# Delta heads: three runs of projections per slot, keys projected after the gate, a last merge level of 64 columns, weight turns moved

## The chip, the core and the metric

The kernel runs on one core of one Trainium2 chip. The metric is the device time of the whole kernel in microseconds (us), as the median of several runs. Times inside an execution are read from one profiled execution.

## What is computed

The program is one decoder layer of three blocks: a gated delta-rule attention, a cross attention and a feed-forward block with experts. The change touches the first block alone, and in it the part that runs over the heads. Cut to what matters here, the reference of it is

```
q = silu(conv4(x @ Wq.T)); k = silu(conv4(x @ Wk.T)); v = silu(conv4(x @ Wv.T))
g = exp(-exp(A_log) * softplus(x @ Wa.T + dt_bias)); beta = sigmoid(x @ Wb.T)
q = q / norm(q); k = k / norm(k)          # per head, 16 heads of 128
for t in time:                            # S is 128 x 128 per head and sequence
    e = v[t] - g[t] * (k[t] @ S)
    S = g[t] * S + outer(k[t], beta[t] * e)
    o[t] = q[t] @ S
o = rmsnorm(o) * norm_w * silu(x @ Wg.T)
return o @ Wo.T
```

There are 4 sequences of 512 tokens and 16 heads. The kernel does not step through time. It cuts time into 4 chunks of 128 tokens, and in each chunk solves a triangular system: with L the 128 x 128 lower triangle of scaled key products, it needs the inverse of (1 + L), once per head, chunk and sequence.

## The kernel before

**Slots.** `delta_heads` is a software pipeline of slots. Slot (i, c) finishes chunk c of head i for all 4 sequences at once, and beside it prepares later chunks. There are 3 slots that only fill the pipeline, a loop over the heads 0 to 14 with 4 slots each, and 4 slots of the last head. Each engine has its own in-order program of the slot, in the function `slot` of its block, and the engines meet in counting semaphores. So the order in which calls stand in each `slot` is the order of the work; no planner changes it. n = 4i + c numbers the slots.

**Projections.** x @ W for one chunk and one of the four weights (K, V, Q, G) is `project` (L526): 128 x 512 outputs (128 channels, 4 sequences of 128 tokens), 4 blocks of the input width, and 3 matmuls per block, because x and W are split into a leading and a remaining part; 12 matmuls in all. K and V share one bank of `gd_PJ`, Q and G share the other (`W_BANK`). Slot n projects K for chunk n + 2, and Q, V and G for chunk n + 1. ACT copies a result out and starts the convolution (`copy_pre`, two instructions), DVE adds the three other taps (`tap`), ACT applies silu (`silu`). For K, DVE then takes the squared norms (`gd_diag`, `gd_kss`), ACT the root (`gd_klen`), DVE the scales, and DVE makes the triangle `gd_Lo`. In the kernel before, K and Q are each projected in two runs of 6 matmuls, V in runs of 3 and 9, G in one run of 12, with other work between.

**The inverse.** Blocks of 16 x 16 on the diagonal are inverted on POOL (`solve`). They go there and back by DMAs on SP's queue: store the triangle, fetch its blocks (`fetch_blocks`, L458), solve, write T and W (the inverse and its transpose), and load them (`spread`). Then three merge levels with block sizes 16, 32 and 64 complete the inverse. A level l is a chain over PE and DVE:

`spread_rows(l)` on PE (W by Lo into bank 2), `masked(l)` on DVE (gives Y), `merge(l)` on PE (Y by T into bank 3), `merged(l)` on DVE (adds into W), and for l < 2 `turn_inverse(l)` on PE (transposes W) and `inverse_rows(l)` on DVE (updates T).

All three levels use the full 128 x 128 Lo and T as the stationary operand, and 64 moving columns.

**The rest of a slot** on PE: `ks` (S by k), `oi` (S by q), `u` (W by R, the corrected values; R is made on DVE from ks and the scaled values Vb), the transposes of v, q and k, `kk` and `qk` (key and query products), `o_sum` and `s_sum` (output and new state), the transpose of o. In slots c = 0 there is no old state, so ks, oi and R are missing.

**Weights.** SP loads the raw weights of the next head. PE transposes them (`turn_weights`, 4 transposes into the bank of that weight), ACT takes the leading part (`lead_weights`), DVE the rest (`rest_weights`), and only then is the bank free and the weight usable. Before, K is turned near the end of slot c = 1, V near the end of c = 2, Q early in c = 3 and G near the end of c = 3, just before the G projection that uses it.

**Two lines that a reader of the trace needs.** An f32 matmul of two f32 operands is recorded as two instructions, so that a group over the 4 sequences reads x8 (a transpose reads x4). Helpers hold the lines: L533 is every projection matmul, L543 every product of `each`, L548 every transpose of `turned`, L524 the turning of weights.

Of the kernel before, what the change touches and what calls it, by code (L numbers as in the profile page):

```python
# [5 lines left out]
ALU = mybir.AluOpType  # L6
# [6 lines left out]
P = 128  # L13
# [307 lines left out]
NM = len(MERGE)  # L321
MERGE_AT = NLV - NM


def delta_heads(nc, xn_parts, A, const_dram, ptab, osq, og_dram, lo_dram, images_dram, rows_dram):
# [10 lines left out]
    with ExitStack() as ctx:  # L336
# [182 lines left out]
        def _(pe):  # L519
# [7 lines left out]
            def project(j, cm, ks, done):  # L527

                bank = PJ[:, W_BANK[j], :].rearrange("p (b t) -> p b t", b=B)
                for k in ks:  # L530
# [4 lines left out]
                    if k == KT - 1:  # L535
                        mm.then_inc(done, 1)
# [14 lines left out]
            def slot(i, c, back, has1, has2, has3, more):  # L551
                n = i * CH + c
                par, parm = c % 2, (c + 1) % 2
                h2, c2 = (i if c < 2 else i + 1), (c + 2) % CH
                h1, c1 = (i if c < 3 else i + 1), (c + 1) % CH
                k_c, q_c, k_m, q_m = of(kT, par), of(qT, par), of(kT, parm), of(qT, parm)
# [3 lines left out]
                def spread_rows(l):  # L560
# [6 lines left out]
                    each(half[2], tiles(Lo_c), [second(W_c, MERGE[l])[:, b] for b in range(B)], y_sum)  # L567

                def merge(l):
# [5 lines left out]
                    each(half[3], tiles(T_c), [Y[:, l % 2, b, :] for b in range(B)], wup)  # L575
# [7 lines left out]
                if back:  # L583
                    spread_rows(0)
                if has2:
                    pe.wait_ge(v_pre, n + 3)
                    pe.wait_ge(w_copied, h2 * 4 + JK + 1)
                    if c == CH - 1:
                        pe.wait_ge(w_copied, h1 * 4 + JV + 1)
                    project(JK, c2, (0, 1), k_proj)  # L590
                if back and c > 0:
                    pe.wait_ge(s_ready, n + 1)
                    each(Bk[1], k_c, tiles(S), ks_done)
                if back:
                    merge(0)
                if has2:
                    project(JK, c2, (2, 3), k_proj)
# [3 lines left out]
                if back:  # L601
                    pe.wait_ge(v_silu, n + 1)
                    pe.wait_ge(kd_ready, n + 1)
                    turned(Bk[5], [vT[:, b * P:(b + 1) * P] for b in range(B)], v_turned)
                    turn_inverse(0)
                    spread_rows(1)
                if has1:
                    pe.wait_ge(g_silu, n + 2)
                    pe.wait_ge(w_copied, h1 * 4 + JQ + 1)
                    project(JQ, c1, (0, 1), q_proj)  # L610
                if back:
                    merge(1)
                if has1:
                    project(JQ, c1, (2, 3), q_proj)
                if back:
                    turn_inverse(1)
# [5 lines left out]
                if back:  # L622
                    spread_rows(2)
# [2209 lines left out]
```

## Time and profile before

| | us |
|---|---|
| median of 3 runs | 3859.66 (3859.34 to 3862.22) |
| the profiled execution, its own time | 3863.27 |
| span of the profiled execution | 3861.5 |
| stage of the delta heads in it (157 to 1840 of the span) | 1683 |
| PE busy over the span | 3359.5 (87%) |
| DVE, ACT, POOL busy | 2143.7 (56%), 1850.7 (48%), 1540.3 (40%) |

The profile is one execution. Its own time is 3.6 us over the median of the runs shown. Busy shares are averages over stages with different limits, and matmuls overlap in the record, so a busy PE is not yet a PE at its peak. PE is the matmul, PEld the loading of its stationary operand; the time from the start of one matmul group to the start of the next says what the group costs.

### The profile page before, as it was taken

The numbers are of one execution on the slowest core, as the hardware profiler recorded it, in microseconds if no ns is written. First come the engines' busy times: TensorE is split into PE (matmuls) and PEld (weight loads), VectorE is DVE, ScalarE is ACT, GpSimd is POOL, SyncE is SP. The second block draws the span as 40 slices with busy tenths as digits, with TensorE's granted clock in tenths as the row PEclk, the third lists the DMA queues.
The fourth block names the chain that finished last, engine by engine and source line by source line (L and its number), as shares of the span: only waits on it lengthen the run. The fifth ranks groups of instructions, "written<-read, shape, count | busy, mean of one in ns | idle before, by whom it ended". The sixth has DMA issues, their size and how long they took to land. (4 is left out here: it accounts for less than half of the span.)

```text
span 3861.5 us, 61617 instructions
## 1 busy us (share of the span) xinstructions
PE 3359.5 (87%) x19269; PEld 2648.6 (69%) x19300; DVE 2143.7 (56%) x4562; ACT 1850.7 (48%) x4568; POOL 1540.3 (40%) x3055
## 2 busy tenths in 40 slices
PE   3699999999999999999894788699969999964993
PEld 2588888888888888888672444388846667653441
DVE  3476676676676676665325677555454644621223
ACT  2466666666666666665210455434433534531110
POOL 2567677667667667674001000155540000003103
PEclk9799999999999999999897899899989999985996
DMA  2222222222222222221443100133362021034325
GB/s 53 77 65 61 69 54 60 70 64 61 70 64 61 70 63 61 66 57 40 153 131 139 61 14 14 39 96 112 100 234 94 27 76 54 33 130 164 123 89 159
DMA packets 432119, 311.55 MB, mean 81 GB/s; under 512 B 131392, under 2 KB 348608, under 8 KB 430816
## 3 DMA queue, kind: packets, MB, share of 16 engines
q1 hardware_dynamic: 424544, 288.99, 25.0%
q0 software_dynamic: 5120, 16.78, 1.3%
q10 hardware_dynamic: 2304, 4.20, 0.3%
q14 instruction: 108, 0.88, 0.1%
q8 instruction: 43, 0.70, 0.1%
HBM read 195.99 MB, written 113.90 MB: 80 GB/s over the span
## 5 line engine op out<-in xcount | busy, mean ns | idle before, releaser
L533 PE MATMUL gd_PJ<-xn_lead,gd_w_rest 128*128 128x512 f32 x1024 | 443.8, 433 | 20.5 <-DVE gd_w_rest L687 20.5
L533 PE MATMUL gd_PJ<-xn_lead,gd_w_lead 128*128 128x512 f32 x1024 | 405.6, 396 | 0.0
L533 PE MATMUL gd_PJ<-xn_rest,gd_w_lead 128*128 128x512 f32 x1024 | 401.8, 392 | 0.0
L694 DVE SCALAR_TENSOR_TENSOR gd_conv<-gd_pre,gd_cur_a,gd_conv 128x512 f32<-128x512 f32 x384 | 298.0, 776 | 90.3 <-ACT gd_conv L842 83.5
L959 POOL TENSOR_TENSOR gd_T<-gd_T,gd_prod 32x14 f32<-32x14 f32 (+6 forms) x896 | 305.8, 341 | 70.2
L956 POOL TENSOR_TENSOR gd_prod<-gd_L,gd_T 32x14 f32<-32x14 f32 (+6 forms) x896 | 299.7, 334 | 70.2
L533 PEld LDWEIGHTS gd_PJ<-xn_lead,gd_w_rest 128*128 128x128 f32 x1024 | 195.4, 191 | 51.0 <-DVE gd_w_rest L687 26.1
L533 PEld LDWEIGHTS gd_PJ<-xn_lead,gd_w_lead 128*128 128x128 f32 x1024 | 193.4, 189 | 45.6
L2505 POOL MEMSET ms_rank<- 128x1 f32 x8 | 0.3, 98 | 554.7 <-POOLq L55 554.7
L533 PEld LDWEIGHTS gd_PJ<-xn_rest,gd_w_lead 128*128 128x128 f32 x1024 | 195.6, 191 | 26.3
L543 PEld LDWEIGHTS gd_B<-gd_Y,gd_T 128*128 128x128 f32 x1536 | 196.2, 191 | 15.4 <-issue 4.1
L2215 PE MATMUL sa_B<-sa_kT,sa_qT 128*128 128x512 f32 (+3 forms) x512 | 179.2, 473 | 30.9 <-DMA sa_qT<-turned_queries_keys 18.0
L2279 ACT ACTIVATE sa_E<-sa_B,sa_nmax 128x512 f32<-128x512 f32 (+3 forms) x256 | 132.4, 525 | 151.8 <-DVE sa_nmax L2329 151.8
L543 PE MATMUL gd_B<-gd_W,gd_Lo 128*128 128x64 f32 x1536 | 195.0, 270 | 7.5 <-DMA gd_T<-inverse_image 7.3
L543 PEld LDWEIGHTS gd_B<-gd_W,gd_Lo 128*128 128x128 f32 x1536 | 187.5, 192 | 10.4 <-issue 7.5
L543 PE MATMUL gd_B<-gd_Y,gd_T 128*128 128x64 f32 x1536 | 193.8, 269 | 0.5 <-DVE gd_Y L707 0.5
L841 ACT COPY gd_pre<-gd_PJ 128x512 f32<-128x512 f32 x192 | 111.9, 583 | 163.6 <-PE gd_PJ L533 156.6
L713 DVE TENSOR_TENSOR gd_W<-gd_W,gd_B 128x256 f32<-128x256 f32 x192 | 80.5, 419 | 190.5 <-PE gd_B L543 190.1
L1452 POOL TENSOR_TENSOR xt_xt<-x_xres,x_bpb 128x512 f32<-128x512 f32 x16 | 20.4, 1281 | 367.7 <-DVE xt_y L1668 306.9
L1860 PE MATMUL sp_B<-sp_w_lead,sp_h_rest 128*128 128x512 f32 x384 | 157.2, 409 | 11.3 <-POOL sp_h_rest L1991 11.3
L2265 PE MATMUL sa_B<-sa_wo_lead,sa_o_parts 128*128 128x512 f32 x512 | 158.7, 390 | 8.9 <-issue 8.9
L694 DVE SCALAR_TENSOR_TENSOR gd_conv<-gd_pre,gd_cur_k,gd_conv 128x512 f32<-128x512 f32 x192 | 146.8, 765 | 16.2 <-ACT gd_conv L842 13.8
(401 smaller groups left out, 8839.2 us busy)
## 6 DMA issues: line engine op xcount, KB each, us to landing
turned_queries_keys<-f_wq SPq DMA_DIRECT2D x16, 1280.0 KB, 6.0
gd_row_sums<-decay_sums SPq DMA_DIRECT2D x64, 256.0 KB, 3.6
triangles<-gd_Lo SPq DMA_DIRECT2D x64, 256.0 KB, 3.4
gd_W<-turned_image SPq DMA_DIRECT2D x64, 256.0 KB, 2.8
gd_T<-inverse_image SPq DMA_DIRECT2D x64, 256.0 KB, 3.3
gated_outputs<-gd_og SPq DMA_DIRECT2D x64, 256.0 KB, 2.7
go_ogt<-gated_outputs SPq DMA_DIRECT2D x16, 1024.0 KB, 6.8
sa_qT<-turned_queries_keys SPq DMA_DIRECT2D x16, 1024.0 KB, 5.6
```

The lines of the kernel that those rows point to most:

```text
L533: mm = pe.matmul(bank, w_parts[wp][:, j, k, :], rhs, start=(k == 0 and wp == 1), stop=(k == KT - 1 and wp + xp == 0))
L543: mm = pe.matmul(bank[:, b, :], lhs[b], rhs[b], start=True, stop=True)
L694: nc.vector.scalar_tensor_tensor(out=conv[:, j], in0=pre[:, parm, j, :, d:d + P], scalar=cur[:, 4 * j + d:4 * j + d + 1], in1=conv[:, j], ...
L713: nc.vector.tensor_tensor(second(W_c, s), second(W_c, s), half[3].rearrange("p b (g m) -> p b g m", m=s), ALU.add).then_inc(w_ready, 1)
L841: nc.scalar.copy(pre[:, parm, j, :, 3:3 + P], bank)
L956: nc.gpsimd.tensor_tensor(prod[:, rows, 0:j], L16[:, rows, j:j + 1].to_broadcast(shape), T16[:, j:j + 1, 0:j].to_broadcast(shape), ALU.mul ...
L959: nc.gpsimd.tensor_tensor(T16[:, rows, 0:j], T16[:, rows, 0:j], prod[:, rows, 0:j], ALU.subtract).then_inc(solving, 1)
L1452: nc.gpsimd.tensor_tensor(xt[:, par, :], xres[:, bass.ds(t, 1), :].rearrange("p o d -> p (o d)"), bpb[:, :], ALU.add).then_inc(bias_ready, 1)
L1860: mm = pe.matmul(bank[:, :], h_parts[hp][:, s, k, :], w_parts[wp][:, k, j, :], start=(k == 0 and hp == 1), stop=(k == KT - 1 and hp + wp = ...
L2215: pe.matmul(Bk[bank][:, col:col + w], qT[:, h, i * P:(i + 1) * P], kT[:, h // REP, 0:w], start=True, stop=False)
L2265: mm = pe.matmul(Bk[i][:, :], part(o_parts, h, op)[:, i * P:(i + 1) * P], wo_parts[wp][:, h, :], start=(h == 0 and op == 1), stop=(h == HE ...
L2279: ex = nc.scalar.activation(E[:, par, E_AT[i]:E_AT[i] + w], Bk[bank][:, col:col + w], ACT.Exp, bias=nmax[:, par, i:i + 1], accum_out=sums[ ...
```

## The change

Nothing is computed otherwise. The parts are:

1. **Three runs of projections per slot.** Q and V are each projected in one run of 12. K moves to right behind G, so that G and K make one run of 24. In slot n it is then for chunk n + 3; ACT's copy of it stays where it was, at the start of a slot, so it is now done in slot n + 1.
2. **The last merge level has 64 columns.** For l = 2 only the lower left 64 x 64 block is new. So the stationary operands are cut to 64 columns (`Lo_c[:, b, 0:TOP]`, `T_c[:, b, 0:TOP]`), PE writes 64 partitions, DVE's `masked(2)` is a multiplication by -1 and `merged(2)` a copy, both of 64 partitions and still 256 elements each.
3. **Weight turns moved.** Q to the very start of slot c = 3, K from the end to the middle of c = 1 (behind the Q projection), G from the end to the middle of c = 3 (before the V projection). V stays at the end of c = 2. ACT's and DVE's parts move with them.
4. **Order of the rest.** On PE the transpose of q now stands before `u`. On DVE the first two taps of K stand between `masked(0)` and `merged(0)`, the first tap of Q comes before `gd_diag`, and `merged(2)` comes after the scales. On ACT the root of the key norms comes before `oi`, and the V copy before the copy of U.

The diff, cut to its core:

```diff
+TOP = MERGE[-1]
...
-            def project(j, cm, ks, done):
+            def project(j, cm, done):
...
+                h3, c3 = (i if c < 1 else i + 1), (c + 3) % CH
...
-                    each(half[2], tiles(Lo_c), [second(W_c, MERGE[l])[:, b] for b in range(B)], y_sum)
+                    if l < NM - 1:
+                        each(half[2], tiles(Lo_c), [second(W_c, MERGE[l])[:, b] for b in range(B)], y_sum)
+                    else:
+                        each(half[2][0:TOP], [Lo_c[:, b, 0:TOP] for b in range(B)], [W_c[:, b, TOP:P] for b in range(B)], y_sum)
...
-                if has2:
-                    project(JK, c2, (2, 3), k_proj)
                 if back and more and c == CH - 1:
                     pe.wait_ge(g_silu, n + 2)
                     turn_weights(h1, JQ)
                 if back:
+                    spread_rows(0)
+                    if c > 0:
+                        pe.wait_ge(s_ready, n + 1)
+                        each(Bk[1], k_c, tiles(S), ks_done)
                     pe.wait_ge(v_silu, n + 1)
                     pe.wait_ge(kd_ready, n + 1)
                     turned(Bk[5], [vT[:, b * P:(b + 1) * P] for b in range(B)], v_turned)
-                    turn_inverse(0)
-                    spread_rows(1)
+                    merge(0)
                 if has1:
                     pe.wait_ge(g_silu, n + 2)
                     pe.wait_ge(w_copied, h1 * 4 + JQ + 1)
-                    project(JQ, c1, (0, 1), q_proj)
+                    project(JQ, c1, q_proj)
+                if back and more and c == 1:
+                    pe.wait_ge(k_pre, n + 3)
+                    turn_weights(i + 1, JK)
...
+                if back and more and c == CH - 1:
+                    pe.wait_ge(q_pre, n + 2)
+                    turn_weights(h1, JG)
...
-                    project(JV, c1, (0,), v_proj)
+                    project(JV, c1, v_proj)
                 if back:
                     merge(2)
                 if has1:
-                    project(JV, c1, (1, 2, 3), v_proj)
+                    pe.wait_ge(q_silu, n + 2)
+                    if back:
+                        pe.wait_ge(vb_ready, n + 1)
+                    turned(Bk[5], q_m, q_turned)
...
-                    project(JG, c1, (0, 1, 2, 3), g_proj)
+                    project(JG, c1, g_proj)
+                if has3:
+                    pe.wait_ge(v_pre, n + 4)
+                    if c == 2 or not back:
+                        pe.wait_ge(w_copied, (i + 1) * 4 + JV + 1)
+                    else:
+                        pe.wait_ge(w_copied, h3 * 4 + JK + 1)
+                    project(JK, c3, k_proj)
...
+                    if l == NM - 1:
+                        nc.vector.tensor_scalar(Y[0:TOP, l % 2], half[2][0:TOP], -1.0, None, ALU.mult).then_inc(y_ready, 1)
+                        return
...
+                    if l == NM - 1:
+                        nc.vector.tensor_copy(W_c[0:TOP, :, TOP:P], half[3][0:TOP]).then_inc(w_ready, 1)
+                        return
```

**Order on PE around the last merge level, before** (slot c = 1; the matmuls of V stand where the line of dots is; gd_Y,gd_T is `merge(2)`, gd_R,gd_W is `u`, gd_cst,gd_qT the transpose of q):

```order
L543 MATMUL gd_B<-gd_Y,gd_T 128x64 [waits gd_t]
L543 MATMUL gd_B<-gd_Y,gd_T 128x64 x3
L533 MATMUL gd_PJ<-xn_lead,gd_w_rest 128x512
...
L543 MATMUL gd_B<-gd_R,gd_W 128x128 [waits gd_oi,gd_w]
L543 MATMUL gd_B<-gd_R,gd_W 128x128 x3
L548 MATMUL gd_B<-gd_cst,gd_qT 128x128 [waits gd_vb,gd_qsilu]
```

Now, at the same place:

```order
L543 MATMUL gd_B<-gd_Y,gd_T 64x64 [waits gd_t]
L543 MATMUL gd_B<-gd_Y,gd_T 64x64 x3
L548 MATMUL gd_B<-gd_cst,gd_qT 128x128 [waits gd_vb,gd_qsilu]
L548 MATMUL gd_B<-gd_cst,gd_qT 128x128 x3
L543 MATMUL gd_B<-gd_R,gd_W 128x128 [waits gd_oi,gd_w]
L543 MATMUL gd_B<-gd_R,gd_W 128x128 x3
```

The nine V matmuls between `merge(2)` and `u` have gone to before `merge(2)`, and the four transposes of q have come in.

**Order on PE around the second merge level, now** (slot c = 1 or 2; in the kernel before, six Q matmuls stand between `merge(1)` and the transpose of W, which is gd_cst,gd_W):

```order
L543 MATMUL gd_B<-gd_kT 128x128 [waits gd_lo,gd_ksilu]
L543 MATMUL gd_B<-gd_kT 128x128 x3
L573 REGISTER_ALU
L577 ISA [waits gd_y]
L543 MATMUL gd_B<-gd_Y,gd_T 128x64 [waits gd_t]
L543 MATMUL gd_B<-gd_Y,gd_T 128x64 x3
L619 REGISTER_ALU
L543 MATMUL gd_B<-gd_S,gd_qT 128x128 [waits gd_r]
L543 MATMUL gd_B<-gd_S,gd_qT 128x128 x3
L548 MATMUL gd_B<-gd_cst,gd_W 128x128 [waits gd_w]
```

The transpose of W is now separated from `merge(1)` by `oi` (gd_S,gd_qT) alone, which a slot c = 0 does not have.

**Order on DVE, now**, from the second level on (slot c = 2; gd_Y is `masked`, gd_W `merged`, gd_T `inverse_rows`):

```order
L730 COPY gd_T<-gd_B 128x16x16 [waits gd_tup]
L715 TENSOR_TENSOR gd_Y<-gd_B,gd_cst 128x256 [waits gd_ysum]
L699 SCALAR_TENSOR_TENSOR gd_conv<-gd_pre,gd_cur_a,gd_conv 128x512 [waits gd_qpre,gd_qhalo]
L764 TENSOR_TENSOR gd_diag<-gd_B,gd_cst 128x512 [waits gd_kk]
L724 TENSOR_TENSOR gd_W<-gd_W,gd_B 128x8x32 [waits gd_wup]
L769 TENSOR_REDUCE gd_kss<-gd_diag 128x4 [waits gd_kdiag]
```

`merged(1)` now waits behind a tap of Q and gd_diag; before, it stood behind two taps of K, and gd_diag came after it.

## Rows read from the trace of the kernel before

**Rows 1.** Windows of four slots of one head (c = 1, 2, 3, 0), us.

```profile
core 0: us, PE busy (x) PEld busy (x) DVE busy (x) ACT busy (x) POOL busy (x), PEclk, DMA share, GB/s
921.36:947.88 26.52, 26.36 (x180) 23.70 (x181) 18.37 (x41) 18.11 (x45) 19.36 (x45) 1.00 0.23 55
947.88:974.20 26.32, 26.18 (x182) 23.59 (x181) 18.36 (x42) 17.94 (x44) 19.16 (x45) 1.00 0.23 54
974.20:1002.81 28.61, 27.10 (x186) 24.14 (x185) 19.37 (x43) 19.93 (x46) 17.32 (x44) 1.00 0.20 50
1002.81:1026.70 23.89, 23.89 (x162) 21.21 (x160) 15.94 (x33) 14.62 (x37) 18.39 (x43) 1.00 0.33 99
```

**Rows 2.** Waits of the weight loads in the slots; us, times, longest.

```profile
PEld gd_PJ L533 <- DVE gd_w_rest L687: 26.1, 30, 1.2
PEld gd_B L548 <- ACT gd_qT L846: 15.2, 47, 0.3
PEld gd_B L543 <- ACT gd_kT L846: 12.1, 61, 0.3
```

**Rows 3.** Timeline of PE in the slot c = 3; start, us, instruction [idle before].

```profile
980.54 0.60 PE L548 MATMUL gd_B<-gd_cst,gd_W 128*128 128x128 f32 x4
980.98 1.00 PE L543 MATMUL gd_B<-gd_W,gd_Lo 128*128 128x64 f32 x8
...
997.97 0.60 PE L548 MATMUL gd_B<-gd_cst,gd_kT 128*128 128x128 f32 x4
999.53 0.50 PE L533 MATMUL gd_PJ<-xn_lead,gd_w_rest 128*128 128x512 f32 x1 [0.96 <-DVE gd_w_rest L687]
```

**Rows 4.** Timeline of PE, slot c = 1, and its last instructions.

```profile
922.28 0.48 PE L533 MATMUL gd_PJ<-xn_lead,gd_w_rest 128*128 128x512 f32 x1
...
923.76 1.05 PE L543 MATMUL gd_B<-gd_S,gd_kT 128*128 128x128 f32 x8
924.64 1.00 PE L543 MATMUL gd_B<-gd_Y,gd_T 128*128 128x64 f32 x8
925.46 0.48 PE L533 MATMUL gd_PJ<-xn_lead,gd_w_rest 128*128 128x512 f32 x1
...
932.36 0.60 PE L548 MATMUL gd_B<-gd_cst,gd_W 128*128 128x128 f32 x4
932.98 1.16 PE L543 MATMUL gd_B<-gd_kT 128*128 128x128 f32 x8
933.98 1.00 PE L543 MATMUL gd_B<-gd_W,gd_Lo 128*128 128x64 f32 x8
...
939.43 1.05 PE L543 MATMUL gd_B<-gd_R,gd_W 128*128 128x128 f32 x8
940.62 0.66 PE L548 MATMUL gd_B<-gd_cst,gd_qT 128*128 128x128 f32 x4
...
944.59 0.48 PE L533 MATMUL gd_PJ<-xn_lead,gd_w_rest 128*128 128x512 f32 x1
...
947.45 0.60 PE L548 MATMUL gd_B<-gd_cst,gd_o 128*128 128x128 f32 x4
```

**Rows 5.** Groups by line with shapes, PEld: a 32-column load, a 128-column load.

```profile
L235 PEld LDWEIGHTS ga_psAB<-xnT,ga_wabT 128*32 128x32 f32 x16 | 1.6, 109 | 3.9 <-issue 3.8
...
L543 PEld LDWEIGHTS gd_B<-gd_W,gd_Lo 128*128 128x128 f32 x1536 | 187.5, 192 | 10.4 <-issue 7.5 <-DMA gd_T<-inverse_image 2.5
```

**Rows 6.** Timeline of DVE, slot c = 1.

```profile
925.68 0.42 DVE L713 TENSOR_TENSOR gd_W<-gd_W,gd_B 128x256 f32<-128x256 f32 x1 [2.75 <-PE gd_B L543]
...
942.31 2.38 DVE L694 SCALAR_TENSOR_TENSOR gd_conv<-gd_pre,gd_cur_a,gd_conv 128x512 f32<-128x512 f32 x3 [1.34 <-ACT gd_conv L842]
```

**Rows 7.** Timeline of ACT, slot c = 1.

```profile
927.61 0.78 ACT L842 ACTIVATE gd_conv<-gd_PJ,gd_cur_k 128x512 f32<-128x512 f32 x1
```

**Rows 8.** Timeline of SP's queue, slot c = 1.

```profile
922.10 0.32 SPq L458 DMA_DIRECT2D gd_L<-triangles  x1
...
946.23 0.32 SPq L458 DMA_DIRECT2D gd_L<-triangles  x1
```

More of the change, by code:

```diff
@@ L622, in slot @@
                 if back:
-                    spread_rows(2)
+                    merge(1)
                     if c > 0:
@@ L722, in slot @@
                     masked(0)
-                    merged(0)
-                if back and more and c == CH - 1:
-                    rest_weights(h1, JQ)
-                if back:
-                    inverse_rows(0)
-                    masked(1)
                 if has2:
@@ L731, in slot @@
                     dve.wait_ge(k_pre, n + 3)
-                    tap(n + 2, par, PK, cur_k, (0, 1), k_tap)
+                    tap(n + 2, par, PK, cur_k, (0,), k_tap)
+                if back and more and c == CH - 1:
+                    rest_weights(h1, JQ)
+                if has2:
+                    tap(n + 2, par, PK, cur_k, (1,), k_tap)
                 if back:
-                    merged(1)
+                    merged(0)
                 if has2:
@@ L744, in slot @@
                 if back:
-                    inverse_rows(1)
+                    inverse_rows(0)
+                    masked(1)
+                if has1:
+                    dve.wait_ge(q_halo, n + 2)
+                    dve.wait_ge(q_pre, n + 2)
+                    tap(n + 1, parm, PQ, cur_a, (0,), q_tap)
+                if back and more and c == 1:
+                    rest_weights(i + 1, JK)
                 if has2:
@@ L749, in slot @@
                 if back:
-                    masked(2)
+                    merged(1)
                 if has2:
@@ L780, in slot @@
                     st.then_inc(lo_ready, 1)
+                if back and more and c == CH - 1:
+                    rest_weights(h1, JG)
                 if has1:
@@ L870, in slot @@
                     copy_pre(parm, PQ, JQ, cur_a, q_pre)
+                if back and more and c == 1:
+                    lead_weights(i + 1, JK)
+                if has2:
+                    act.wait_ge(k_len, n + 3)
+                    nc.scalar.activation(klen[:, :], kss[:, :], ACT.Sqrt).then_inc(k_root, 1)
                 if back and c > 0:
```

86 lines of the change are left out of this document (32 added, 54 removed).

## The prediction

> **What bounds the kernel now.** I read the slot windows first [rows 1]. In each slot PE is busy for all but 0 to 1.5 us, at the full granted clock (1.00, the level of 2.4 GHz), while DVE, ACT and POOL are busy 15 to 20 us of a slot of 24 to 29 us. One head takes 26.52 + 26.32 + 28.61 + 23.89 = 105.3 us and 16 heads 1685 us, the stage that the table names. So PE's program, with the waits inside it, is the time. Everything else matters only through what PE waits for. Next, the waits of the weight loads [rows 2], which show a stalled PE better than the matmuls do: 26.1 us for the remaining part of turned weights, 15.2 us for the silu of q, 12.1 us for the silu of k. Last, the timeline of PE, read from start to start: a group of 64 moving columns costs 925.46 - 924.64 = 0.82, one of 128 columns 0.88, a run of 6 projection matmuls 1.48, one of 12 matmuls 2.86, all [rows 4], and four transposes 980.98 - 980.54 = 0.44 [rows 3].
>
> **Part 1, joined runs.** Two runs of 6 cost 2 x 1.48 = 2.96, one of 12 costs 2.86 [rows 4]: entering a run costs 0.10. A slot goes from seven runs (2 K, 2 Q, 2 V, 1 G) to three, which is 4 x 0.10 = 0.4 us, **1.6 us per head**. No wait of PE is put into it: the matmuls are the same 48.
>
> **Part 2, 64 columns in the last level.** The two groups of this level now load 64 instead of 128 stationary columns, eight loads each; moving columns stay at 64. No row shows a 64-column load. The nearest are 32 columns at 109 ns and 128 columns at 192 ns [rows 5], 0.86 ns a column, which puts 64 columns at 137 ns, 55 ns less. Whether that shortens the group depends on what paces it: 0.82 us over 8 is 0.10 us each, close to 128 x 0.86 = 0.11, so I take it that loads pace it. At 0.055 each the group would cost 8 x 0.055 plus some 0.05 on leaving it, 0.49, a gain of 0.33. The bounds are 0 (the moving side paces it) and 8 x 0.055 = 0.44. I take 0.32, being nearest to the load rate: twice per slot, **2.6 us per head**, with 0 and 3.5 as ends. DVE's two operations keep 256 elements a partition and their 0.42 us [rows 6].
>
> The Trainium skill states in "TensorE: Matmul & The Clock Gate", section on LDWEIGHTS, that a load takes its columns divided by 1.2 in ns, and that rows do not matter. By it a load falls from 107 to 53 ns, 0.43 per group, and the forecast would be 14 us lower; the slope of the rows agrees with it, the lengths in the rows are longer.
>
> **Part 3, waits that go.** Weights are waited for in c = 3 alone, twice, 26.1 / 15 = 1.74 us a head [rows 2]. The longest, 1.2, stands before the G projection: 999.53 - 997.97 = 1.56 for four transposes [rows 3]. The other 0.54 stands before Q. Q is now turned at the slot's start, some 3 us before its use, and G before the V run, with V's 2.86 and seven more groups between. The silu of q comes late by 0.30 in c = 1 to 3 (940.62 - 939.43 = 1.19 against 0.88) [rows 4]. In the new order the table load and the root stand ahead of oi, so that ACT has q ready around the end of the V run. The silu of k is late by 0.18 here (932.98 - 932.36 against 0.44) and makes the product of keys 1.00 instead of 0.88 [rows 4]; K now is projected a slot earlier and its taps come first on DVE, 2 us before that product. The stage's sum is 26.1 + 15.2 + 12.1 = 53.4, plus 0.1 x 61 for the slowed product, 60 us, **3.8 us per head**.
>
> **Part 4, waits that come.** From the start of a merge group to DVE's start takes 925.68 - 924.64 = 1.04 [rows 4, 6], DVE takes 0.42, and I allow 0.07 for passing the word to PE, an estimate without a row (0 to 0.18, the smallest wait above): 1.53 from group start to release. The group itself covers 0.82, so PE needs 0.71 of other work, or waits.
> - `u` after `merge(2)`: before, nine V matmuls covered it. Now four transposes do, 0.44. Wait 0.28, in all four slots: 1.12. A shorter group shortens both sides alike.
> - c = 0 has no ks: between `spread_rows(0)` and `merge(0)` stand the transposes of v, 0.44, again 0.28.
> - c = 0 has no oi: nothing stands between `merge(1)` and the transpose of W, and on DVE a tap (2.38 / 3 = 0.79 [rows 6]) and gd_diag stand ahead of `merged(1)`. About 0.8.
> - c = 1 to 3: oi covers 0.88. masked(1) ends 0.25 before `merge(1)` starts (0.82 + 0.88 against 1.04 + 0.42), so tap, diag and merged (0.79 + 0.65 + 0.42 from there) end 1.6 after its start, due at 1.70: just in time. In c = 1 the rest of K's weights is put in front: a wait of 0.56. (Diag and rest are taken at 0.65 each, between merged's 0.42 and the tap's 0.79, as operations of 512 elements with simpler arithmetic than the tap.)
> - c = 3: `masked(0)`, a tap and Q's rest end at 1.04 + 0.42 + 0.79 + 0.65 = 2.9; Q is due at 0.82 + 0.88 + 0.44 + 0.82 = 2.96. About 0.1.
>
> Together 2.85; as several hand-overs are met with 0.1 to spare, I add 0.1 a slot: **3.25 us per head**, with ends 2.85 and 5 (a DVE or ACT that is 0.4 us late in each slot).
>
> **What costs nothing, and why.** The turns of weights are the same number, only elsewhere; SP's loads of raw weights wait for all four turns, of which the last now comes earlier. SP's ring of triangle, fetch, solve and load ran from fetch to fetch in 946.23 - 922.10 = 24.1 us in a slot of 26.5 [rows 8], part of it waiting. The new slot would be 25.1 on average, and the triangle is ready some 3 us earlier in the slot, so the ring stays hidden by 1 us or more. If it did not, the slots c = 0 would show it first.
>
> **The sum.** -1.6 - 2.6 - 3.8 + 3.25 = -4.75 us per head, times 16 is -76 us. The profiled execution took 3863.3, so 3787; it stands 3.6 over the median of the runs, which gives 3784. I forecast **3785 us**, 1.9% under 3859.7.
>
> **Rivals.**
> 1. *The narrow loads are no faster* (the moving side, or a fixed cost, paces the group). For it: no row has this shape. Against it: 0.10 each is the load rate. Part 2 is gone, 2.6 x 16 = 41 us: **3826 us**.
> 2. *Changing the width costs a drain.* PE would empty before a group of other width begins: four changes a slot. A group of eight is recorded as 1.00 us but costs 0.82 [rows 4], so 0.18 of overlap is what a drain could lose; 4 x 0.18 x 64 = 46 us, which more than eats part 2: **3831 us**. Against it: in the stage groups of other kinds follow one another without such a gap. The Trainium skill states in "TensorEngine Tiling (Array Packing)", section on tiling modes, that a change of tiling mode drains TensorE; no row shows whether 64 stationary columns on 128 rows count as such a mode. By that rule this is the case that comes.
> 3. *Slower: K's chain becomes the slot's.* ACT copies K only after the silu of the gate and the squares of o; behind it on DVE stand two taps of K, and only then `merged(0)`, for which PE's transpose of W waits. That transpose is due at 0.82 + 0.88 + 0.44 + 0.82 + 2.86 = 5.8 us into the slot; two taps, merged and hand-over take 1.58 + 0.42 + 0.07, so K's copy may come as late as 3.7. I expect it at about 1.2: K's run ends 0.44 before the slot, and two copies of at most 0.78 each follow [rows 7]. ACT is busy 18 to 20 of 26 us, so lateness is possible. It decides from 3.7 - 1.2 = 2.5 us on; the gain is gone at 2.5 + 76/64 = 3.7 us. At 4.3 us late it is (4.3 - 2.5) x 64 - 76 = +39: **3899 us**.
> 4. *The waits only move.* The waits of part 3 return behind other weights and silus: +60 us, with part 1, 2 and 4 as said, **3845 us** if all return; with part 2 failing too, 3886.
>
> **How the numbers follow.** Forecast 0.71, rival 1 0.11, rival 2 0.07, rival 3 0.05, rival 4 0.06 (half of it near or beyond no change). The likeliest case gives 3785. Its own ends are 3765 (part 2 at 3.5 and part 4 at 2.85: -6.05 a head, -97 us) and 3812 (part 4 at 5: -3.0 a head, -48 us). The range reaches to rivals 1 and 2: 3765 to 3832. A measurement of this kernel can tell about 0.2%, 8 us, from no change. Faster 0.91, within it 0.03, slower 0.06.
>
> **What would show it.** Slots of about 25.5 (c = 1), 25.0, 25.6 and 23.9 (c = 0). PE: a run of 24 of 5.6 us; no wait for gd_w_rest above 0.1 but in c = 1; the wait for gd_qT gone; a new wait for gd_W at `u` of 0.3 in every slot. The 64x64 groups at 0.5: at 0.8 rival 1 is right; wide groups beside them lengthened by 0.1 to 0.2 mean rival 2. If the transposes of W after `merge(0)` wait for DVE, and K's copy starts over 3 us into the slot, it is rival 3. The forecast is wrong in its core if PE's waits in the stage sum to over 100 us.

## The result, and the profile after

| | before | change |
|---|---|---|
| median, us | 3860.94 (3859.34 to 3865.22, 4 runs) | 3816.81 (3810.25 to 3819.29, 4 runs) |
| ratio | | 0.9881, interval 0.9864 to 0.9898 |
| profiled execution, span | 3861.5 | 3815.6 |
| one head in steady state | 105.37 | 102.13 |
| delta heads, first projection to the first matmul of the output block | 1729.2 | 1679.8 |

The change gained 44 us, 1.1%. The forecast was 76: the sign and the range held (3816.81 lies in 3765 to 3832), but two fifths of the expected gain are missing. It also lies above 3812, where the forecast's likeliest case ended, in the part of the range that reached over to rivals 1 and 2.

The slots again, windows of one head (c = 1, 2, 3, 0); they answer to [rows 1]:

```profile
core 0: us, PE busy (x) PEld busy (x) DVE busy (x) ACT busy (x) POOL busy (x), PEclk, DMA share, GB/s
901.97:927.89 25.92, 25.92 (x183) 22.89 (x181) 18.03 (x41) 18.05 (x43) 19.41 (x45) 1.00 0.22 56
927.89:953.60 25.71, 25.71 (x183) 22.86 (x182) 17.96 (x41) 18.44 (x44) 19.79 (x46) 1.00 0.25 55
953.60:979.66 26.06, 26.06 (x186) 23.25 (x185) 18.87 (x42) 18.55 (x45) 15.60 (x40) 1.00 0.21 55
979.66:1004.10 24.44, 23.85 (x162) 20.65 (x161) 16.79 (x33) 16.73 (x39) 21.93 (x45) 1.00 0.34 100
```

The forecast had 25.5, 25.0, 25.6 and 23.9. These four add up to 100.0, while the forecast's sum, 4.75 less than 105.3, is 100.6: 0.6 of the 2.1 us that are missing against the slots is an error between the two. All four slots are 0.4 to 0.7 longer than forecast, about evenly, and PE is busy throughout in three of them. That is not how one late engine looks. It looks like a price paid in every slot.

Waits of the weight loads in the slots (us, times, longest), for [rows 2]:

```profile
PEld gd_B L543 <- issue: 32.4, 125, 0.4
PEld gd_B L548 <- DVE gd_W L724: 13.6, 31, 0.7
...
PEld gd_B L543 <- DVE gd_W L722: 10.6, 63, 0.6
PEld gd_B L543 <- DVE gd_Y L715: 6.0, 17, 0.7
```

All three rows of before are gone: no wait for turned weights, for q or for k. Three waits on DVE have come, 30 us together where 53 went. The first row is the strange one: 125 times, two per slot, the load stands idle and waits for nothing that the profile shows. In the kernel before it was there 14 times, 3.8 us in all.

Timeline of PE, slot c = 2 (start, us, instruction), for [rows 4]:

```profile
927.89 1.00 PE L543 MATMUL gd_B<-gd_W,gd_Lo 128*128 128x64 f32 x8
928.73 1.11 PE L543 MATMUL gd_B<-gd_S,gd_kT 128*128 128x128 f32 x8
929.68 0.60 PE L548 MATMUL gd_B<-gd_cst,gd_vT 128*128 128x128 f32 x4
930.11 1.00 PE L543 MATMUL gd_B<-gd_Y,gd_T 128*128 128x64 f32 x8
930.92 0.48 PE L534 MATMUL gd_PJ<-xn_lead,gd_w_rest 128*128 128x512 f32 x1
931.24 0.39 PE L534 MATMUL gd_PJ<-xn_rest,gd_w_lead 128*128 128x512 f32 x1
...
937.79 0.60 PE L548 MATMUL gd_B<-gd_cst,gd_W 128*128 128x128 f32 x4
938.32 0.68 PE L543 MATMUL gd_B<-gd_W,gd_Lo 128*64 128x64 f32 x8
938.93 0.50 PE L534 MATMUL gd_PJ<-xn_lead,gd_w_rest 128*128 128x512 f32 x1
939.27 0.39 PE L534 MATMUL gd_PJ<-xn_rest,gd_w_lead 128*128 128x512 f32 x1
...
941.56 0.39 PE L534 MATMUL gd_PJ<-xn_lead,gd_w_lead 128*128 128x512 f32 x1
941.88 0.68 PE L543 MATMUL gd_B<-gd_Y,gd_T 128*64 128x64 f32 x8
942.49 0.66 PE L548 MATMUL gd_B<-gd_cst,gd_qT 128*128 128x128 f32 x4
943.07 1.16 PE L543 MATMUL gd_B<-gd_R,gd_W 128*128 128x128 f32 x8
944.06 1.06 PE L543 MATMUL gd_B<-gd_qT,gd_kT 128*128 128x128 f32 x8
...
947.58 0.48 PE L534 MATMUL gd_PJ<-xn_lead,gd_w_rest 128*128 128x512 f32 x1
...
953.16 0.60 PE L548 MATMUL gd_B<-gd_cst,gd_o 128*128 128x128 f32 x4
```

Read from start to start. The run of 24 takes 953.16 - 947.58 = 5.58 (forecast 5.6). The narrow groups take 0.61 each, not the forecast 0.5. What stands beside them is longer too: the transposes of W ahead of the first take 938.32 - 937.79 = 0.53 instead of 0.44, and the last projection ahead of the second takes 941.88 - 941.56 = 0.32 where others take 0.23. And S,kT takes 929.68 - 928.73 = 0.95, where before it took 0.88.

The two load shapes, groups by line (times, busy, mean ns), for [rows 5]:

```profile
L543 PEld LDWEIGHTS gd_B<-gd_Y,gd_T 128*128 128x128 f32 x1024 | 125.3, 193 | 6.1 <-DVE gd_Y L715 6.0
...
L543 PEld LDWEIGHTS gd_B<-gd_W,gd_Lo 128*64 128x64 f32 x512 | 34.6, 137 | 10.7 <-issue 10.7
```

A load of 64 columns takes the 137 ns that the interpolation gave.

The new waits: in c = 0 on PE at the second merge level, with DVE's operations beside it, and DVE's `merged(2)` in c = 2.

```profile
987.17 1.00 PE L543 MATMUL gd_B<-gd_Y,gd_T 128*128 128x64 f32 x8
988.68 0.66 PE L548 MATMUL gd_B<-gd_cst,gd_W 128*128 128x128 f32 x4 [0.51 <-DVE gd_W L724]
```

```profile
987.42 0.68 DVE L764 TENSOR_TENSOR gd_diag<-gd_B,gd_cst 128x512 f32<-128x512 f32 x1
988.21 0.42 DVE L724 TENSOR_TENSOR gd_W<-gd_W,gd_B 128x256 f32<-128x256 f32 x1
...
942.60 0.42 DVE L722 COPY gd_W<-gd_B 64x256 f32<-64x256 f32 x1 [0.95 <-PE gd_B L543]
```

`merged(1)` starts 1.04 after its group, as in [rows 6]; gd_diag had ended 0.1 before, so DVE's queue does not bind there. It ends at 988.63 and PE goes on at 988.68: the hand-over that the forecast put at 0.07 without a row is 0.05. At `u` the same: 942.60 + 0.42 = 943.02, PE at 943.07.

Last, the chain of K and the ring of SP, for [rows 7, 8]. ACT in c = 3, DVE in c = 3, SP's queue:

```profile
953.46 0.56 ACT L857 COPY gd_pre<-gd_PJ 128x512 f32<-128x512 f32 x1
953.93 0.78 ACT L858 ACTIVATE gd_conv<-gd_PJ,gd_cur_k 128x512 f32<-128x512 f32 x1
```

```profile
957.44 0.41 DVE L724 TENSOR_TENSOR gd_W<-gd_W,gd_B 128x256 f32<-128x256 f32 x1
```

```profile
924.27 0.32 SPq L459 DMA_DIRECT2D gd_L<-triangles  x1
...
949.13 0.32 SPq L459 DMA_DIRECT2D gd_L<-triangles  x1
```

ACT takes K just before the slot begins (953.60), and is done with its second copy 1.1 us into it (the forecast's point was 3.7 for the end of that copy). `merged(0)` ends at 957.85, 2.1 us before the transpose of W needs it. The ring turns once per slot, here in 24.9 us, and PE waits for none of its loads.

### The profile page after: what moved, and what is told of

It reads as the page before. It is cut to its first block and busy times, and to the rows that moved or that the text cites. A ratio compares the mean times of both kernels' runs of the same rounds, so it can differ in the third digit from the quotient of the medians.

```text
span 3815.6 us, 61633 instructions
## 1 busy us (share of the span) xinstructions
PE 3332.3 (87%) x19300; PEld 2601.2 (68%) x19300; DVE 2142.5 (56%) x4562; ACT 1866.6 (49%) x4568; POOL 1576.9 (41%) x3055
## 5 line engine op out<-in xcount | busy, mean ns | idle before, releaser
L534 PE MATMUL gd_PJ<-xn_lead,gd_w_rest 128*128 128x512 f32 x1024 | 421.4, 411 | 0.0
L534 PE MATMUL gd_PJ<-xn_lead,gd_w_lead 128*128 128x512 f32 x1024 | 403.0, 394 | 0.0
L534 PE MATMUL gd_PJ<-xn_rest,gd_w_lead 128*128 128x512 f32 x1024 | 401.3, 392 | 0.0
L977 POOL TENSOR_TENSOR gd_T<-gd_T,gd_prod 32x14 f32<-32x14 f32 (+6 forms) x896 | 314.2, 351 | 70.2
L974 POOL TENSOR_TENSOR gd_prod<-gd_L,gd_T 32x14 f32<-32x14 f32 (+6 forms) x896 | 285.2, 318 | 70.2
L534 PEld LDWEIGHTS gd_PJ<-xn_lead,gd_w_lead 128*128 128x128 f32 x1024 | 193.4, 189 | 43.8
L534 PEld LDWEIGHTS gd_PJ<-xn_lead,gd_w_rest 128*128 128x128 f32 x1024 | 194.2, 190 | 37.4
L534 PEld LDWEIGHTS gd_PJ<-xn_rest,gd_w_lead 128*128 128x128 f32 x1024 | 194.5, 190 | 35.3
L833 DVE SCALAR_TENSOR_TENSOR gd_og<-gd_B,ptab,gd_gate 128x512 f32<-128x512 f32 x64 | 48.0, 751 | 248.4 <-PE gd_B L548 248.4
L543 PEld LDWEIGHTS gd_B<-gd_Y,gd_T 128*128 128x128 f32 (+1 forms) x1536 | 159.9, 174 | 28.9 <-issue 22.2
L543 PE MATMUL gd_B<-gd_W,gd_Lo 128*128 128x64 f32 (+1 forms) x1536 | 172.8, 256 | 5.4 <-DMA gd_T<-inverse_image 5.4
L543 PE MATMUL gd_B<-gd_Y,gd_T 128*128 128x64 f32 (+1 forms) x1536 | 174.4, 257 | 2.6 <-DVE gd_Y L715 1.0
L699 DVE SCALAR_TENSOR_TENSOR gd_conv<-gd_pre,gd_cur_k,gd_conv 128x512 f32<-128x512 f32 x192 | 163.9, 854 | 20.9 <-ACT gd_conv L858 19.1
L543 PEld LDWEIGHTS gd_B<-gd_W,gd_Lo 128*128 128x128 f32 (+1 forms) x1536 | 159.8, 174 | 16.5 <-issue 16.5
```

The costliest lines, as they stand in the source:

```text
L534: mm = pe.matmul(bank, w_parts[wp][:, j, k, :], rhs, start=(k == 0 and wp == 1), stop=(k == KT - 1 and wp + xp == 0))
L543: mm = pe.matmul(bank[:, b, :], lhs[b], rhs[b], start=True, stop=True)
L699: nc.vector.scalar_tensor_tensor(out=conv[:, j], in0=pre[:, parm, j, :, d:d + P], scalar=cur[:, 4 * j + d:4 * j + d + 1], in1=conv[:, j], ...
L974: nc.gpsimd.tensor_tensor(prod[:, rows, 0:j], L16[:, rows, j:j + 1].to_broadcast(shape), T16[:, j:j + 1, 0:j].to_broadcast(shape), ALU.mul ...
L977: nc.gpsimd.tensor_tensor(T16[:, rows, 0:j], T16[:, rows, 0:j], prod[:, rows, 0:j], ALU.subtract).then_inc(solving, 1)
```

## The experiments

Totals are medians of 4 runs (10 for the narrow level in the kernel before) where an interval is given, and else one run. The kernel before ran beside them at 3863 to 3868 us, and the ratios are to it. The head's period, a mean over 12 heads of the profiled execution, separates effects that totals can't. The edits shift the lines of some kernels, so that L544, L549 and L534 in their rows are the helpers at L543, L548 and L533 of the kernel before. From head to head it stays within 0.3 us in the change and in most experiments, and within 0.4 to 0.8 in the two kernels of the old order and in the two best ones.

**The last level wide again** (all the rest as changed):

```diff
-each(half[2][0:TOP], [Lo_c[:, b, 0:TOP] for b in range(B)], ...
+each(half[2], [Lo_c[:, b, 0:128] for b in range(B)], ...
-each(half[3][0:TOP], [T_c[:, b, 0:TOP] for b in range(B)], ...
+each(half[3], [T_c[:, b, 0:128] for b in range(B)], ...
```

> The changed kernel with part 2 undone on PE: the last level again loads 128 columns and writes 128 partitions (DVE still works on 64). Theory A (the narrow groups pay for a change of width): in the trace of the change a narrow group costs 0.61 instead of 0.81, but the interval before it is 0.09 longer and the first interval after it 0.02 to 0.06 longer; undoing it then costs about 0.24 us a slot, 0.9 us a head: a head of 103.0 against 102.1, about 15 us more than the change. Theory B (part 2 gives what was predicted, 0.64 a slot, and the shortfall lies elsewhere): a head of 104.7, 41 us more. Theory C (part 2 is worth nothing): a head of 102.1, no difference.

Measured: 3835.14 us, ratio 0.9917 (0.99 to 0.9933); 103.42 us per head. The "issue" row is gone, the wait at `u` has grown from 10.6 to 18.8:

```profile
PEld gd_B L543 <- DVE gd_W L722: 18.8, 62, 0.3
PEld gd_B L548 <- DVE gd_W L724: 13.7, 31, 0.7
```

So part 2 is worth 1.29 us a head, and 18 us in all by the medians (14 by the ratios): half of what was forecast, and more than the 0.9 of theory A. By the starts of the single matmuls, which the timeline merges, 0.8 of it is direct. The rest comes over `u`: DVE gets the narrow group's result 0.72 after its start (942.60 - 941.88) instead of 1.04, while PE leaves the group only 0.22 earlier.

**The last level narrow, in the kernel before** (part 2 alone, DVE's two operations included):

```diff
+TOP = MERGE[-1]
-each(half[2], tiles(Lo_c), [second(W_c, MERGE[l])[:, b] for b in range(B)], y_sum)
+if l < NM - 1:
+    each(half[2], tiles(Lo_c), [second(W_c, MERGE[l])[:, b] for b in range(B)], y_sum)
+else:
+    each(half[2][0:TOP], [Lo_c[:, b, 0:TOP] for b in range(B)], [W_c[:, b, TOP:P] for b in range(B)], y_sum)
```

> The kernel before with part 2 alone. Theory A: 0.2 us a group gained, half of it given back at the borders: 0.2 to 0.25 us a slot, 0.9 us a head (105.35 to about 104.4), 3846 us. Theory B: 2.6 us a head, 3820 us. Theory C: 105.35, 3861 us.

Measured: 3866.91 us, ratio 1.0003 (0.9993 to 1.0013), 105.33 us per head against 105.37. Part 2 alone gives nothing, as only theory C had it. Waits of the weight loads, same columns as [rows 2]:

```profile
PEld gd_B L544 <- issue: 22.0, 60, 0.4
PEld gd_B L549 <- ACT gd_qT L859: 18.6, 46, 0.4
PEld gd_B L544 <- ACT gd_kT L859: 12.3, 61, 0.3
PEld gd_B L544 <- DMA gd_T<-inverse_image: 10.5, 14, 1.2
```

The wait for q grows from 15.2 to 18.6 and a wait for the inverse's DMA from 2.5 to 10.5. By the starts of the single matmuls the groups gain 1.7 a head here too and their borders take 1.0 back, much as in the new order. The remaining 0.7 goes to the two waits: 0.2 to q, and the rest to the load of the inverse, above all at the change from c = 0 to c = 1. So in the old order these slots were held by chains of other engines, and a shorter PE program waited longer for them. The forecast took its parts as a sum; part 2 is worth something only with the rest of the new order. Which of parts 1, 3 and 4 frees it was not tried one by one.

**96 columns instead of 64** (changed kernel, both groups of the last level):

```diff
-each(half[2][0:TOP], [Lo_c[:, b, 0:TOP] for b in range(B)], ...
+each(half[2][0:96], [Lo_c[:, b, 0:96] for b in range(B)], ...
-each(half[3][0:TOP], [T_c[:, b, 0:TOP] for b in range(B)], ...
+each(half[3][0:96], [T_c[:, b, 0:96] for b in range(B)], ...
```

> The changed kernel with 96 stationary columns in the last level instead of 64 (32 rows of the output are not used). A load of 96 columns should take about 165 ns, between 137 and 192, and pace the group at 0.084 each: a group of about 0.65. Theory A1 (the border cost belongs to the half array, 64 columns or fewer): no border cost at 96, so about 0.05 us a slot better than 64 columns: a head of 101.9. Theory A2 (any change of width costs the border): the border cost stays and the gain is smaller than at 64: a head of 102.3 to 102.5.

Measured: 3812.86 us, ratio 0.9857 (0.984 to 0.9873), 101.83 us per head, 0.30 less than with 64 columns although each load is longer. PE around the second transpose of W, and the load's group:

```profile
935.80 0.60 PE L548 MATMUL gd_B<-gd_cst,gd_W 128*128 128x128 f32 x4
936.23 0.81 PE L543 MATMUL gd_B<-gd_W,gd_Lo 128*96 128x64 f32 x8
```

```profile
L543 PEld LDWEIGHTS gd_B<-gd_W,gd_Lo 128*96 128x96 f32 x504 | 49.3, 164 | 0.0
```

The transposes take 936.23 - 935.80 = 0.43 again, the projection ahead of `merge(2)` 0.23, the idle time behind "|" is 0.0, and the "issue" row is gone. Thus the border is a price of the width 64, not of any width under 128. This is rival 2, at a smaller price than it had. By the starts of the single matmuls in the change the narrow group costs 0.09 on the interval before it, 0.05 on its first (0.107 instead of 0.058) and 0.07 on its last (0.151 instead of 0.084). The first interval of what follows is 0.02 longer for a run of projections and 0.05 longer for four transposes (0.165 instead of 0.117).

The Trainium skill states in "TensorEngine Tiling (Array Packing)", Tiling Modes, that "Changing tiling mode (not just tile) drains the TensorE", and lists 128 x 64 as a mode, but no width of 96. The trace agrees on both: a border at 64 columns, none at 96. That the border is this drain is the page's word; no run here shows the mode itself.

**V in two runs around `merge(2)`** (changed kernel; `project` given a range of blocks):

```diff
-                    project(JV, c1, v_proj)
+                    project(JV, c1, v_proj, (0, 1))
                 if back:
                     merge(2)
                 if has1:
+                    project(JV, c1, v_proj, (2, 3))
```

> The changed kernel with the V projection in two runs of 6, the second behind the last merge group, as cover for DVE's copy before u. In the change PE waits about 0.2 us for that copy in every slot. Theory A (the wait is real and covered by any work of 0.3 us or more): the wait of PE for gd_W at u goes, an entry into a run comes, 0.06 to 0.1: 0.1 us a slot gained, a head of 101.7, 6 us less than the change. Rival (the entry costs as much as the wait did, or v becomes late for the next slot): a head of 102.1 or more.

Measured: 3804.84 us, ratio 0.9847 (0.983 to 0.9863), 101.62 us per head. Six matmuls now cover DVE between `merge(2)` and `u`:

```profile
937.96 0.60 PE L549 MATMUL gd_B<-gd_cst,gd_qT 128*128 128x128 f32 x4
938.39 1.06 PE L544 MATMUL gd_B<-gd_R,gd_W 128*128 128x128 f32 x8
939.29 0.94 PE L544 MATMUL gd_B<-gd_qT,gd_kT 128*128 128x128 f32 x7
```

The transposes of q are back at 0.43 and R,W at 0.90, against 0.58 and 0.99. So the wait at `u` costs 0.24 a slot, and entering one run more costs less: 0.51 a head is left. Joining V into one run was the wrong side of this trade.

**G turned at its old place** (changed kernel; PE's transposes, ACT's and DVE's parts back to the end of c = 3):

```diff
-                if back and more and c == CH - 1:
-                    pe.wait_ge(q_pre, n + 2)
-                    turn_weights(h1, JG)
                 if has1:
...
+                if back and more and c == CH - 1:
+                    pe.wait_ge(q_pre, n + 2)
+                    turn_weights(h1, JG)
                 if back and more and c == 2:
```

> The changed kernel with G's weights turned where they were before, after the state product at the end of slot c = 3. Theory A (the moved turn is what took the 1.2 us wait away): the wait for gd_w_rest before the G run comes back, about 1.2 us once a head, a head of 103.3 against 102.1. Rival (the rest of the new order has given DVE and ACT room, so that the late turn no longer costs): a head of 102.1 to 102.4.

Measured: 3831.4 us (one run), 103.34 us per head; slot c = 3 takes 27.37 instead of 26.07, the others stay within 0.04.

```profile
979.99 0.60 PE L548 MATMUL gd_B<-gd_cst,gd_kT 128*128 128x128 f32 x4
981.55 0.50 PE L534 MATMUL gd_PJ<-xn_lead,gd_w_rest 128*128 128x512 f32 x1 [0.96 <-DVE gd_w_rest L692]
```

The wait of [rows 3] is back to the digit, 1.56 for four transposes. This one moved turn is worth 1.21 us a head, 18 us by the period and 15 by the totals: more than a third of the whole gain. The other turns and the chains of q and k have no experiment of their own.

**Transposes of v before S,kT** (changed kernel):

```diff
                     spread_rows(0)
-                    if c > 0:
-                        pe.wait_ge(s_ready, n + 1)
-                        each(Bk[1], k_c, tiles(S), ks_done)
...
                     turned(Bk[5], [vT[:, b * P:(b + 1) * P] for b in range(B)], v_turned)
+                    if c > 0:
+                        pe.wait_ge(s_ready, n + 1)
+                        each(Bk[1], k_c, tiles(S), ks_done)
```

> The changed kernel with the transposes of v before the product of S and k instead of behind it, the same instructions. Theory A (a group of 128 moving columns that stands directly behind one of 64 pays 0.055 us in its first interval, 0.165 instead of 0.11; behind four transposes it does not): 0.055 a slot with c above 0, a head of 101.93 against 102.09. Rival (the 0.165 belongs to the group itself, or to its semaphore): 102.09.

Measured: 3809.95 us (one run), 101.96 us per head.

```profile
926.64 0.61 PE L548 MATMUL gd_B<-gd_cst,gd_vT 128*128 128x128 f32 x4
927.09 1.06 PE L543 MATMUL gd_B<-gd_S,gd_kT 128*128 128x128 f32 x8
927.98 1.00 PE L543 MATMUL gd_B<-gd_Y,gd_T 128*128 128x64 f32 x8
```

S,kT falls from 0.95 to 0.89, the transposes stay at 0.45: the neighbour ahead made the difference, not S or k. The total is one run inside the change's own spread; the period carries the verdict, 0.05 for each slot that has an S,kT.

**96 columns and V in two runs together:**

```diff
-each(half[3][0:TOP], [T_c[:, b, 0:TOP] for b in range(B)], ...
+each(half[3][0:96], [T_c[:, b, 0:96] for b in range(B)], ...
...
-                    project(JV, c1, v_proj)
+                    project(JV, c1, v_proj, (0, 1))
                 if back:
                     merge(2)
                 if has1:
+                    project(JV, c1, v_proj, (2, 3))
```

> The changed kernel with 96 stationary columns in the last level and V in two runs of 6 around the last merge group. Theory A (the two gains are of different kinds and add): the wait before u, 0.33 in the 96-column kernel, goes for an entry of 0.1: a head of 100.9 from 101.83, about 3797 us. Rival (the waits move on to another engine, as they did in the kernel before with narrow groups): a head of 101.5 or more.

Measured: 3793.92 us, ratio 0.9811 (0.9793 to 0.983), 100.78 us per head. The two gains alone would have given 102.13 - 0.30 - 0.51 = 101.32. Of the other 0.54, 0.38 is what 96 columns had lost at `u` (there the wait had risen from 10.6 to 19.4 in the stage, since DVE gets the result later): with six matmuls behind `merge(2)` it is covered. Another 0.11 is the last interval of `merge(2)`, 0.057 ahead of a projection and 0.085 ahead of the transposes.

**All covers:** that version, with a first block of Q before `merge(0)` and a first block of V before the second transpose of W in c = 0, and in c = 1 the rest of K's weights behind `merged(1)` on DVE:

```diff
+                    if c == 0:
+                        pe.wait_ge(g_silu, n + 2)
+                        pe.wait_ge(w_copied, h1 * 4 + JQ + 1)
+                        project(JQ, c1, q_proj, (0,))
                     merge(0)
...
+                    else:
+                        pe.wait_ge(k_pre, n + 3)
+                        pe.wait_ge(w_copied, h1 * 4 + JV + 1)
+                        project(JV, c1, v_proj, (0,))
                     turn_inverse(1)
...
-                if back and more and c == 1:
-                    rest_weights(i + 1, JK)
...
                     merged(1)
+                if back and more and c == 1:
+                    rest_weights(i + 1, JK)
```

> As the run with 96 columns and V in two, and three more covers: in slots c = 0 the first three Q matmuls stand before merge(0) and the first three V matmuls before the second transpose of W, and in c = 1 DVE makes the rest of K's weights after merged(1) instead of before. Theory A (PE's waits in c = 0, 0.34 and 0.70, and 0.16 in c = 1, are hand-overs to DVE that other work covers): 1.1 us a head less, 99.8, about 3780 us. Rival (DVE or ACT is late itself, the waits stay or move): a head above 100.5.

Measured: 3776.86 us, ratio 0.9776 (0.9753 to 0.9799), 100.0 us per head, 0.8 less than in the version before it, where 1.1 was expected; c = 0 takes 23.27 on average instead of 24.11 there. Waits of the weight loads on DVE's W and on the inverse's DMA, in the slots:

```profile
PEld gd_B L549 <- DVE gd_W L734: 3.5, 16, 0.7
PEld gd_B L544 <- DMA gd_T<-inverse_image: 3.3, 10, 0.5
```

Nearly all waits are gone. The load of the inverse shows again, as in the kernel before, but not in the change: the last group of c = 0 takes 0.60 instead of 0.43 and the first of c = 1 0.94 instead of 0.84, which is most of the missing 0.3. The ring may be next.

**The transposes of o between the runs of G and K** (changed kernel, four runs per slot):

```diff
                     project(JG, c1, g_proj)
+                if back:
+                    pe.wait_ge(o_ready, n + 2)
+                    turned(Bk[0], tiles(o), o_turned)
                 if has3:
...
                     project(JK, c3, k_proj)
-                if back:
-                    pe.wait_ge(o_ready, n + 2)
-                    turned(Bk[0], tiles(o), o_turned)
```

> The changed kernel with the four transposes of o between the G and the K projection instead of behind both: one run of 24 becomes two of 12, so that a slot has four runs instead of three. Theory A (what a run's entry costs depends on what stands before it: behind four transposes the first interval is 0.315 instead of 0.23, but the last transpose is followed after 0.03 instead of 0.11, so the entry is free): no change, a head of 102.1. Theory P (the prediction's price, 0.10 for every entry): a head of 102.5.

Measured: 3811.97 us (one run), 102.33 us per head against 102.13: 0.05 a slot, half of the 0.10 that an entry was priced at. The result lies between the two expectations, so neither theory has the price alone.

```profile
926.74 0.60 PE L548 MATMUL gd_B<-gd_cst,gd_o 128*128 128x128 f32 x4
927.09 0.47 PE L534 MATMUL gd_PJ<-xn_lead,gd_w_rest 128*128 128x512 f32 x1
927.40 0.39 PE L534 MATMUL gd_PJ<-xn_rest,gd_w_lead 128*128 128x512 f32 x1
```

The run's first interval is 0.31 instead of 0.23, but the transposes ahead of it take 0.35 instead of 0.44. By these two an entry behind transposes is free. The 0.05 that is lost all the same lies inside the runs: two of 12 take 5.69 together, where one of 24 takes 5.56. Behind a group of 64 moving columns only 0.03 is given back: its last interval is 0.084 ahead of a run and 0.112 elsewhere.

**All covers and the swap of v:**

```diff
                     turned(Bk[5], [vT[:, b * P:(b + 1) * P] for b in range(B)], v_turned)
+                    if c > 0:
+                        pe.wait_ge(s_ready, n + 1)
+                        each(Bk[1], k_c, tiles(S), ks_done)
                     if c == 0:
...
                         project(JQ, c1, q_proj, (0,))
                     merge(0)
```

> The kernel with all covers, and with the transposes of v before the product of S and k. Theory A (the 0.055 of the second experiment on order adds to the covers): 0.16 us a head less, 99.85 from 100.0, about 3775 us. Rival (the slot is now held by another chain, the inverse's DMAs at the change from c = 0 to c = 1): 100.0.

Measured: 3777.54 us, ratio 0.9778 (0.9761 to 0.9794), 99.91 us per head. The total cannot tell it from the version before it. By the starts, S,kT gains 0.06 in each of three slots, as expected, and the last group of c = 0, which the inverse's DMA holds, takes 0.68 instead of 0.60: each expectation is right in half. Both are 1.1% under the change by their ratios (0.9776 against 0.9881) and 2.2% under the kernel before.

## Why the prediction was right, and where it was off

The mechanism was right in the main: PE's program with its waits is the time, and the change cut both. Two of its steps were not: what joining runs does to the groups beside them was put at nothing, and rival 2, weighed as an alternative, was true in part. That the total still fell into the range is owed also to parts 3 and 4, which came out 1.1 a head better than forecast. The sizes, per head:

| step | forecast | measured |
|---|---|---|
| part 1, joined runs | -1.6 | -1.7 in the runs, +1.0 in the groups that now touch: -0.7 |
| part 2, 64 columns | -2.6 | -1.7 in the groups, +0.8 beside them: -0.9 |
| part 3, waits that go | -3.8 | -3.8, and -0.3 for the inverse's DMA: -4.1 |
| part 4, waits that come | +3.25 | +2.5 |
| sum | -4.75 | -3.2; the period shows -3.24 |

The measured column is read from start to start, as means over 12 heads of either kernel. Of the change's own edits only part 2 and the turn of G were undone or tried alone; the waits of part 4 were covered in the experiments on V in two runs and with all covers.

- **Part 1 failed in the sentence "the matmuls are the same 48", which stopped at the runs.** An entry does cost 0.10 in the record of the runs, and 0.42 a slot went, as forecast. But the runs had also stood between other groups, and these now touch. S,kT takes 0.95 for 0.89 and the product of keys 0.95 where 0.89 was expected once its wait had gone, since both stand right behind a group of 64 moving columns. S,qT takes 0.95 for 0.87 and three groups of 64 moving columns 0.84 for 0.81, since no run follows them any more: ahead of a run the last interval had been shorter, so that the 0.10 of an entry was in part paid back by the group ahead. Together this is 0.28 in a slot with old state. The swap of v showed for S,kT that the neighbour does it; for the others it is read from the starts alone.
- **Part 2: the load is 137 ns and its rate in the group 0.058 us, as taken; the term was mis-sized at the edges.** "Some 0.05 on leaving it" was in truth 0.05 on entering, 0.09 on leaving (0.151 for 0.058) and 0.09 on the interval before. Rival 2 was counted as an alternative with a chance of 0.07, and the sign that was named for it, wide groups beside the narrow ones lengthened by 0.1 to 0.2, came at 0.09. It came together with the gain, at some 0.4 a slot instead of 0.72 (0.2 of it beside the groups, as much inside them), so that the gain was cut and not turned over.
- **Part 3** held, waits by name: both waits for weights (1.8), q (1.1), k and the slowed product (0.9). The short waits for the inverse's DMA (0.3) went too; the forecast had left them out. The G turn alone was tried and is 1.21.
- **Part 4** held but for one wait: `u` 0.24 for 0.28, c = 0 0.34 for 0.28 and 0.73 for 0.8. In c = 1 it was 0.2 for 0.56: DVE's tap, rest and diag take 0.69, 0.60 and 0.60 from start to start when they follow one another, not 0.79, 0.65 and 0.65, which is 0.2 of the difference. The rest is PE's four groups there, which take 0.17 more together than the forecast had. Of the 0.1 a slot for hand-overs with no room, 0.05 was used.
- **The multiplication by 16** was generous too. The period counts 15 times, -49 us; filling the pipeline cost 2.5 us more, and the last head gained 2.7. Of the 2.5, 1.8 lie in the first slot (27.8 instead of 26.0), and there the granted clock was 0.86 instead of 0.92: by the trace's clock records it stood at the lower of its two levels for 7.7 us of the slot instead of 4.3. At that level the matmuls of a projection stand 0.43 us apart (129.03, 129.45, 129.88 in the kernel before), at the full one 0.23, so about half of the 3.4 us is lost: the 1.8.
- **Outside the stage** the program lost 3.5 us in the profiled execution: the cross attention took 601.9 instead of 596.6, and the rest gained a little. The change doesn't touch it, and it took 598 to 605 in all experiments. The granted clock accounts for it: over this stage it was 0.98 in the kernel before and in the two experiments at 598 (the narrow level in the kernel before, and V in two runs), and 0.97 in the change and in all others. By the clock records it stood at the lower level for 20 us before and for 31 after, and half of the difference is the 5 us; the stage's time less half of what was spent at the lower level is 585 to 588 in all twelve kernels. Why the clock fell more often is open.

So of the 30 us between forecast and result in the profiled execution, 27 lie in the stage of the heads, where parts 1 and 2 fell short by 2.6 a head and parts 3 and 4 gave 1.1 back, and where the sixteenth head, counted as 4.75, brought almost nothing with the filling; 3.5 lie outside.

Rival 1 is wrong, by the 0.61 of a narrow group and by the 18 us. Rival 3 is wrong: K's copy stood 2.6 us before its point. Rival 4 is wrong in the change (32 us of waits on other engines against 53), but waits that grow are what ate the rest of part 2 alone in the old order.

## What to carry to other kernels

Price an edit on TensorE with its neighbours, interval by interval over the border: moving a group changes what stands beside two others, and a narrower stationary operand can cost at its borders half of what it gains inside. A shorter group is worth something only where the engine is not waiting for a chain; take the waits out first, and count two such gains as a sum only then. Long runs of matmuls are cover: keep a piece behind each hand-over (here 1.5 us from the start of a group of 64 moving columns to PE's release), rather than join them for 0.1 us an entry.

## What the runs showed of the hardware that I had not expected

All from f32 groups at the granted clock 1.00, start to start.

- **64 stationary columns among groups of 128 cost about 0.2 us a group** (0.09 before, 0.05 in the first interval, 0.07 at the end), and the load's wait is shown with no releaser. 96 columns cost nothing at the border. With what it adds to its neighbour ahead a group of 64 costs 0.70, one of 96 0.62 to 0.65. So 96 is the better width here, though its loads follow at half again the distance.
- **Loads pace small groups:** the inner interval is 0.058, 0.085 and 0.112 us for 64, 96 and 128 columns, while the load is recorded as 137, 164 and 192 ns. The Trainium skill, in "TensorE: Matmul & The Clock Gate", section on LDWEIGHTS, gives columns divided by 1.2 in ns, 53, 80 and 107: the intervals agree within 6 ns, the recorded lengths don't.
- **A product of 128 moving columns right behind a group of 64** has a first interval of 0.165 instead of 0.11. Four transposes behind such a group have 0.117, so it is not the 128 moving columns alone. The last interval of the group of 64 is 0.11 there, as inside it, and 0.08 ahead of a run of projections.
- **Entering a run of 512 moving columns** costs 0.08 in its first interval, 0.31 for 0.23, and where transposes or a product of 128 moving columns stand ahead, their last interval is 0.03 instead of 0.11. So the entry is free there by the record, though splitting a run behind transposes cost 0.05 a slot. Behind a group of 64 moving columns 0.03 of it comes back.
